# A macaron transformer layer on one core: probabilities turned by DMA, the work listed by slots, rotation on VectorE, halves of the weighted values summed by TensorE

## The chip, the core and the metric

The kernel runs on one core of a Trainium2 chip. The metric is the device time of one execution in microseconds. The kernel before takes 887.43 us as the median of three runs (884.81 to 891.82).

## What is computed

Sixteen sequences (batches) of 256 rows and 256 features go through half a feed-forward step, an attention step and half a feed-forward step. Every step normalises its input first and adds its result to the rows.

```python
def _layernorm(x, axis=-1, eps=1e-05):
    m = jnp.mean(x, axis=axis, keepdims=True)
    v = jnp.var(x, axis=axis, keepdims=True)
    return (x - m) / jnp.sqrt(v + eps)

def _L0_attn_ref(x, wq, wk, wv, wo):
    B, S, E = x.shape                       # 16, 256, 256
    H, D = (NUM_HEADS, HEAD_DIM)            # 16, 16
    q = apply_rope((x @ wq).reshape(B, S, H, D))
    k = apply_rope((x @ wk).reshape(B, S, H, D))
    v = (x @ wv).reshape(B, S, H, D)
    scores = jnp.einsum('bqhd,bkhd->bhqk', q, k) / math.sqrt(D)
    scores = scores + causal[None, None, :, :]
    attn = jax.nn.softmax(scores, axis=-1)
    return jnp.einsum('bhqk,bkhd->bqhd', attn, v).reshape(B, S, E) @ wo

def _L0_ffn_ref(x, W_up, W_gate, W_down):   # weights 1024 x 256, made ternary
    up = jnp.einsum('bsd,ed->bse', x, ternary_quant(W_up))
    gate = jnp.einsum('bsd,ed->bse', x, ternary_quant(W_gate))
    return jnp.einsum('bse,de->bsd', jax.nn.silu(up) * gate, ternary_quant(W_down))

x = x + 0.5 * _L0_ffn_ref(_layernorm(x), ...)
x = x + _L0_attn_ref(_layernorm(x), ...)
x = x + 0.5 * _L0_ffn_ref(_layernorm(x), ...)
```

Products run in float16. An operand that needs more bits is split into a high part (the value rounded to float16) and a low part (the rest), and both are multiplied.

## The kernel before

All 16 batches lie in SBUF. The unit of work is a **slot**. A full slot holds one **pair** of heads of one batch (128 pairs in all) and one **round** of a feed-forward step (two chunks of 128 hidden units; four rounds a step, 128 in all). Eight slots make a **step**, and in step t batch t is in its first feed-forward (slots 0 to 3), batch t-1 in its projections, batch t-2 in its pairs, and batch t-3 in its second feed-forward (slots 4 to 7). Each engine walks the steps with a list of its own (`PE_SLOT`, `ACT_SLOT`, `DVE_SLOT`, `POOL_SLOT` and the tables of exceptions `_OTHER` and `_EXTRA`), and engines wait for each other by counting semaphores. The order is thus written by hand.

What a **pair** does. TensorE writes the masked scores of both heads to PSUM: 256 columns for the upper half of the queries (rows 128 to 255) and 128 for the lower, since the mask is causal. VectorE takes the negated row maxima (`neg_max`, in SBUF) and multiplies them with the scale (`exp_bias`). ScalarE writes the exponentials (`prob`, float32, 384 columns a head). One slot later TensorE turns `prob` in three 128x128 transposes a head into `probt_ps` (one PSUM tile, so the heads go one after the other). ScalarE writes the high part `prob_h` and, for head 0, a float32 copy `prob_t`. The low part is made by GpSimd for head 0 (`prob_lo_0`, from the copy) and by VectorE for head 1 (`prob_lo_1`). Two slots after the scores TensorE multiplies with v: `v_row` holds per head 16 high columns, 16 low columns and a one, so 33 columns. VectorE inverts the sum (`pv_inverse`), adds the two halves of the weighted values (`pv_add`, into `pv_sum`) and multiplies (`pv_scale`, into `attn`).

What a **round** does. TensorE `up` (eight products of 256 columns) to ScalarE `tanh` to VectorE `silu`; TensorE `gate` (eight) and silu to VectorE `hidden`; ScalarE `hidden_hi` (`hid_h`) and GpSimd `hidden_lo` (`hid_l`); TensorE `down` (eight) in the next slot. `up_ps` and `gate_ps` are one tile each. `ffn_added` adds the sum of four rounds to the rows.

What a **batch** does beside that goes through one PSUM tile `misc_ps` in the order of the list `MISC`: the turning of the normalised rows for the three norms (norm1 and norm2 normalised by GpSimd in two operations, norm3 by VectorE), the projections of q and k (`qk0`, `qk1`: 12 products of 512 columns in all), of v, the turning of `attn` (`attn_t`) and `out_proj`. Of q and k ScalarE takes a copy (`qk_rows`), GpSimd multiplies it with cosine and sine (`rope_mul`, four operations of 512 columns a batch) and adds (`rope_add`); high and low parts go to `q_row` and `k_row`, and SP turns them by DMA (`turn_rows`) into `q_stk` and `k_pad`: 48 blocks of 128x128 a batch.

Within a slot `tanh` stands ahead of most exponentials on ScalarE, and the scores of the next pair wait until the exponentials of the last have read `score_ps`. This ring is scores, v's product, transposes, up, tanh, exponentials.

## Time and profile before

The profiled execution took 886.57 us, of which 884.8 us lie between its first and its last instruction (the span).

| | |
|---|---|
| median of the runs | 887.43 us |
| profiled execution | 886.57 us |
| its span | 884.8 us |
| TensorE busy | 708.4 us (80%), 6976 products |
| VectorE busy | 709.8 us (80%), 1591 instructions |
| ScalarE busy | 620.1 us (70%) |
| GpSimd busy | 557.4 us (63%) |
| DMA queue of SP | 109632 packets, 36.71 MB, 20.0% of 16 engines |
| mean granted TensorE clock | 0.951 |

A share of busy time says how close an engine is to being the limit, not that it is one: an engine that waits its turn in a ring shows as idle. Matmul durations overlap in TensorE's pipeline, so what a matmul costs is read from one start to the next.

### The profile page before, as it was taken

To read this page: it belongs to the slowest core of one execution; us is meant where nothing else is said; L and a number is where in the kernel's file an instruction comes from. 1 tells how busy PE (TensorE), PEld (TensorE's weight loads), DVE (VectorE), ACT (ScalarE), POOL (GpSimd) and SP (SyncE) were. 2 spreads that over 40 slices of the span, in tenths; PEclk is the share of its full clock that TensorE was granted. 3 is DMA by queue.
4 is the path that set the end of the run, shared out by engine and by line. 5 is a ranking of instruction groups with operands and counts; after the bars stand their busy time and mean duration, and the time that the engine had idled before them with its cause. 6 is when DMAs were issued, how large, how long until landed. Compare 5 with 4: busy or idle time off the path is not lost.

```text
span 884.8 us, 18797 instructions
## 1 busy us (share of the span) xinstructions
PE 708.4 (80%) x6976; PEld 584.6 (66%) x6976; DVE 709.8 (80%) x1591; ACT 620.1 (70%) x1365; POOL 557.4 (63%) x568
## 2 busy tenths in 40 slices
PE   0537578888888979898988888897979898767756
PEld 0325366777777868677777777786868777655544
DVE  2753486989998898988898999899898889777663
ACT  2104387878878788878887887878787788767642
POOL 2026685676768676767777676867676767744232
PEclk9968797999999999999999999999999999989798
DMA  8300312030303040302113030303040211213000
GB/s 317 119 1 1 72 29 45 13 66 9 73 13 73 14 72 13 72 14 48 39 21 65 1 73 14 72 14 73 14 72 14 55 31 31 55 29 57 1 13 13
DMA packets 110297, 40.20 MB, mean 45 GB/s; under 512 B 100992, under 2 KB 109440, under 8 KB 109696
## 3 DMA queue, kind: packets, MB, share of 16 engines
q1 hardware_dynamic: 109632, 36.71, 20.0%
q10 hardware_dynamic: 576, 2.29, 0.7%
q8 instruction: 57, 0.93, 0.4%
q14 instruction: 32, 0.26, 0.1%
HBM read 9.63 MB, written 4.19 MB: 16 GB/s over the span
## 4 chain that ended last, share of the span: by engine, by line
ACT 30%; PE 28%; DVE 19%; POOL 12%; issue 9%; DMA 1%; DVEq 0%; POOLq 0%; SPq 0%; ACTq 0%
PE misc_ps L386 7%; ACT prob L639 5%; ACT prob_h L630 5%; ACT tanh_b L648 5%; ACT prob L641 4%; PE pv_ps L435 4%; PE up_ps L386 3%; PE probt_ps L453 3%; POOL hid_l L1027 3%; DVE hid L934 3%; PE misc_ps L500 3%; ACT prob_t L634 3%; DVE silu_b L923 3%; PE score_ps L403 2%; POOL k_row L334 2%
## 5 line engine op out<-in xcount | busy, mean ns | idle before, releaser
L1027 POOL TENSOR_TENSOR hid_l<-hid,hid_h 128x512 f16<-128x512 f32 x128 | 148.5, 1161 | 225.9 <-ACT hid_h L654 210.9
L630 ACT ACTIVATE prob_h<-probt_ps 128x384 f16<-128x384 f32 x256 | 127.5, 498 | 76.5 <-PE probt_ps L453 76.2
L639 ACT ACTIVATE prob<-score_ps,exp_bias,exp_scale 128x256 f32<-128x256 f32 x256 | 147.2, 575 | 2.3 <-DVE exp_bias L874 1.2
L453 PE MATMUL probt_ps<-ident_f,prob 128*128 128x128 f32 x768 | 133.0, 283 | 13.8 <-ACT prob_t L634 13.8
L386 PE MATMUL up_ps<-xt_hi,tern_up 128*128 128x256 f16 x512 | 127.4, 286 | 20.2 <-DVE tern_up L708 13.1
L1020 POOL TENSOR_TENSOR prob_l<-prob_t,prob_h 128x384 f16<-128x384 f32 x128 | 118.1, 923 | 37.0 <-ACT prob_t L634 36.8
L386 PE MATMUL down_ps<-tern_down,hid_h 128*128 128x256 f16 x512 | 121.0, 276 | 19.3 <-POOL hid_l L1027 19.2
L386 PE MATMUL up_ps<-xt_lo,tern_up 128*128 128x256 f16 x512 | 127.4, 286 | 0.0
L386 PE MATMUL gate_ps<-xt_hi,tern_gate 128*128 128x256 f16 x512 | 123.9, 280 | 1.8 <-DVE tern_gate L708 1.8
L386 PE MATMUL gate_ps<-xt_lo,tern_gate 128*128 128x256 f16 x512 | 123.1, 279 | 0.0
L641 ACT ACTIVATE prob<-score_ps,exp_bias,exp_scale 128x128 f32<-128x128 f32 x256 | 121.2, 473 | 0.0
L386 PE MATMUL down_ps<-tern_down,hid_l 128*128 128x256 f16 x512 | 121.0, 276 | 0.0
L923 DVE SCALAR_TENSOR_TENSOR silu_b<-tanh_b,up_ps 128x512 f32<-128x512 f32 x128 | 87.0, 679 | 40.7 <-ACT tanh_b L648 40.2
L654 ACT ACTIVATE hid_h<-hid 128x512 f16<-128x512 f32 x128 | 82.8, 647 | 45.5 <-DVE hid L934 45.5
L648 ACT ACTIVATE tanh_b<-up_ps,tanh_scale 128x512 f32<-128x512 f32 x128 | 88.4, 690 | 33.0 <-PE up_ps L386 32.9
L868 DVE TENSOR_REDUCE neg_max<-score_ps 128x2 f32<-128x512 f32 x128 | 87.4, 683 | 22.5 <-PE score_ps L409 22.4
L453 PEld LDWEIGHTS probt_ps<-ident_f,prob 128*128 128x128 f32 x768 | 90.0, 144 | 21.4 <-issue 17.1
L934 DVE SCALAR_TENSOR_TENSOR hid<-silu_b,gate_ps 128x512 f32<-128x512 f32 x128 | 88.0, 687 | 17.7 <-DVE silu_b L923 0.5
L403 PE MATMUL score_ps<-mask_b,ident_b 128*128 128x256 bf16 x256 | 72.3, 283 | 28.3 <-ACT prob L641 24.9
L435 PE MATMUL pv_ps<-v_row,prob_h 128*128 128x33 f16 x768 | 55.9, 179 | 41.1 <-issue 27.4
L435 PEld LDWEIGHTS pv_ps<-v_row,prob_h 128*128 128x128 f16 x768 | 47.9, 97 | 54.8 <-issue 36.7
L916 DVE TENSOR_TENSOR prob_l<-probt_ps,prob_h 128x384 f16<-128x384 f32 x128 | 70.5, 551 | 14.8 <-ACT prob_h L630 14.6
(101 smaller groups left out, 1868.4 us busy)
## 6 DMA issues: line engine op xcount, KB each, us to landing
xs<-x SPq DMA_DIRECT2D x16, 256.0 KB, 2.8
out<-xs SPq DMA_DIRECT2D x16, 256.0 KB, 2.1
raw_gate<-w_gate_t ACTq DMA_DIRECT2D x1, 1024.0 KB, 7.6
raw_up<-w_up_t SPq DMA_DIRECT2D x1, 1024.0 KB, 7.7
raw_down<-w_down_t SPq DMA_DIRECT2D x1, 1024.0 KB, 10.4
raw_w<-wqkvo ACTq DMA_DIRECT2D x1, 1024.0 KB, 12.5
cos<-rope_cos SPq DMA_DIRECT2D x1, 512.0 KB, 13.6
sin<-rope_sin SPq DMA_DIRECT2D x1, 512.0 KB, 14.4
```

Of the source, the lines that this page charges most:

```text
L386: mm = pe.matmul(dst, lhs, rhs, start=flags and n == 0, stop=n == len(pairs) - 1, skip_group_check=True)
L403: pe.matmul(score_ps[:, j, P:3 * P], ident_b[:, :], mask_b[:, :], start=True, stop=False, skip_group_check=True)
L435: mm = pe.matmul(dst, part[:, pair % 2, j, col * P:(col + 1) * P], v[:, keys, h, :], start=first, stop=True, skip_group_check=True)
L453: mm = pe.transpose(probt_ps[:, n * P:(n + 1) * P], prob[:, pair % 2, j, col * P:(col + 1) * P], ident_f[:, :])
L630: act.activation(prob_h[:, pair % 2, j, :], probt_ps[:, 0:384], ACT.Copy).then_inc(prob_h_done, 1)
L639: act.activation(prob[:, s % 2, j, 0:256], score_ps[:, j, 0:256], ACT.Exp, bias=exp_bias[:, j:j + 1], scale=exp_scale[:, :])
L641: act.activation(prob[:, s % 2, j, 256:384], score_ps[:, j, 256:384], ACT.Exp, bias=exp_bias[:, 2 + j:3 + j], scale=exp_scale[:, :]).then_ ...
L648: act.activation(tanh_b[:, :], up_ps[:, :], ACT.Tanh, scale=tanh_scale[:, :]).then_inc(tanh_done, 1)
L923: dve.scalar_tensor_tensor(out=silu_b[:, :], in0=tanh_b[:, :], scalar=1.0, in1=up_ps[:, :], op0=ALU.add, op1=ALU.mult).then_inc(silu_done, 1)
L934: dve.scalar_tensor_tensor(out=hid[:, s % 2, :], in0=silu_b[:, :], scalar=0.25 / X_SCALE ** 2, in1=gate_ps[:, :], op0=ALU.mult, op1=ALU.mu ...
L1020: pool.tensor_tensor(prob_l[:, pair % 2, 0, :], prob_t[:, pair % 2, :], prob_h[:, pair % 2, 0, :], ALU.subtract).then_inc(prob_l_done[0], 1)
L1027: pool.tensor_tensor(hid_l[:, s % 2, :, :].rearrange("p m n -> p (m n)"), hid[:, s % 2, :], hid_h[:, s % 2, :, :].rearrange("p m n -> p (m ...
```

## The change

The work is listed by a running slot number g instead of by steps, for all engines. Pair n has its scores in slot n. Its parts and its rounds stand as follows.

- The rounds of the first feed-forward of batches 0 to 5 (24 rounds) stand in slots -15 to 8, one after another (`AHEAD = 6`); of later batches b in slots 8(b-6)+17 to +20. The second feed-forward of batch b stands in slots 8b+13 to 8b+16. So slots 13 to 96 have a round each, slots 9 to 12 none, and from 97 on every second group of four has none.
- Probabilities are no longer turned by TensorE. In the next slot ScalarE makes the high part of all 768 columns of the pair in one operation, GpSimd the low part of all 768, and SP turns both (12 blocks) in one DMA into `prob_t`. v's product comes three slots after the scores (`PV_LAG = 3`) instead of two.
- v's product is done in two: 17 columns (high part and the one) and 16 columns (low part), both summed into the same 17 columns of PSUM. There are 24 small products a pair instead of 12, and `pv_add` is gone; `pv_scale` reads PSUM.
- The scores of a half of the queries are one product for both heads (512 and 256 columns, with one product for the mask each). `neg_max` lies in a free corner of the scores' PSUM tile.
- VectorE multiplies q and k with cosine and sine straight from PSUM; the copy by ScalarE is gone.
- `up_ps` and `tanh_b` have two buffers, as the turned rows of norm1 have.
- The order within a slot is one list per engine without exceptions.

```diff
+PE_SLOT = ["scores", "product_v", "misc_a", "up", "gate", "misc_b", "down"]
+ACT_SLOT = ["prob_hi", "misc_a", "tanh", "exps_0", "exps_1", "rope_hi", "misc_b", "hidden_hi"]
+DVE_SLOT = ["row_max", "exp_bias", "pv_inverse", "ffn_added", "pv_scale", "misc_a", "norm_stats", "silu",
+            "norm_mean", "hidden", "norm_var", "norm_apply", "misc_b"]
+POOL_SLOT = ["norm_power", "rope_add", "prob_lo", "row_lo", "norm_apply", "hidden_lo"]
...
+            def turn_probs(n):
+                sp.wait_ge(prob_l_done, n + 1)
+                if n >= 2:
+                    sp.wait_ge(pv_done, n - 1)
+                sp.dma_start_transpose(prob_t[:, n % 2, :, :, :].rearrange("p a c q -> p (a c) q"),
+                                       prob_hl[:, n % 2, :, :].rearrange("p a k -> p (a k)")
+                                       ).then_inc(prob_turned[n % 2], 16)
...
-                            for part in (prob_h, prob_l):
-                                mm = pe.matmul(dst, part[:, pair % 2, j, col * P:(col + 1) * P], v[:, keys, h, :],
-                                               start=first, stop=True, skip_group_check=True)
+                            for part in range(2):
+                                p, head = prob_t[:, n % 2, part, block, :], v[:, keys, 2 * s + j, :]
+                                pe.matmul(dst, p, head[:, 0:HD + 1], start=first, stop=True, skip_group_check=True)
+                                mm = pe.matmul(dst[:, 0:HD], p, head[:, HD + 1:VW], start=False, stop=True,
+                                               skip_group_check=True)
...
+            def exps(n, tile):
+                act.wait_ge(bias_done, n + 1)
+                if tile and n >= 2:
+                    act.wait_ge(prob_l_done, n - 1)
...
+            def prob_hi(n):
+                act.wait_ge(exp_done[0], n + 1)
+                act.wait_ge(exp_done[1], n + 1)
+                if n >= 2:
+                    act.wait_ge(prob_turned[n % 2], 16 * (n // 2))
+                act.activation(prob_hl[:, n % 2, 0, :], prob[:, n % 2, :], ACT.Copy).then_inc(prob_h_done, 1)
...
+                    dve.tensor_tensor(rope_c[:, tile, :], misc_ps[:, :], cos[:, tile, :], ALU.mult)
+                    dve.tensor_tensor(rope_s[:, tile, :], misc_ps[:, :], sin[:, tile, :], ALU.mult
+                                      ).then_inc(misc_taken, 1)
...
-                dve.tensor_tensor(prob_l[:, pair % 2, 1, :], probt_ps[:, 0:384], prob_h[:, pair % 2, 1, :],
-                                  ALU.subtract).then_inc(prob_l_done[1], 1)
...
+            def norm_power(k, b):
+                pool.wait_ge(var_done[k], b + 1)
+                pool.tensor_tensor(rstd[k][:, :], var_s[k][:, :], minus_half[:, :], ALU.pow).then_inc(rstd_done[k], 1)
...
+            def prob_lo(n):
+                pool.wait_ge(prob_h_done, n + 1)
+                pool.tensor_tensor(prob_hl[:, n % 2, 1, :], prob[:, n % 2, :], prob_hl[:, n % 2, 0, :], ALU.subtract
+                                   ).then_inc(prob_l_done, 1)
```

How the rows move on GpSimd, around norm1 and norm2 of a steady batch (slots 5, 6 and 7 of a step). Before, `rstd` of the one norm stands behind a low part and its two applying operations follow in the next slot, and so for the other norm:

```order
L1020 TENSOR_TENSOR prob_l<-prob_t,prob_h 128x384
L977 TENSOR_TENSOR rstd<-var_s,minus_half 128x2
L1027 TENSOR_TENSOR hid_l<-hid,hid_h 128x512
L984 TENSOR_TENSOR centred<-xs,mv 128x512
L988 TENSOR_TENSOR xhat<-centred,rstd 128x512
L1020 TENSOR_TENSOR prob_l<-prob_t,prob_h 128x384
L977 TENSOR_TENSOR rstd<-var_s,minus_half 128x2
L1027 TENSOR_TENSOR hid_l<-hid,hid_h 128x512
L984 TENSOR_TENSOR centred<-xs,mv 128x512
L988 TENSOR_TENSOR xhat<-centred,rstd 128x512
L1020 TENSOR_TENSOR prob_l<-prob_t,prob_h 128x384
L1027 TENSOR_TENSOR hid_l<-hid,hid_h 128x512
```

After, in the places 5 to 7 of a batch, both `rstd` stand at the head of slot 6, ahead of the low part of pair 5 (`prob_hl` is now high and low part in one tensor), and the four applying operations of both norms stand together in slot 7:

```order
L912 TENSOR_TENSOR hid_l<-hid,hid_h 128x512
L871 TENSOR_TENSOR rstd<-var_s,minus_half 128x2 x2
L907 TENSOR_TENSOR prob_hl<-prob,prob_hl 128x768
L912 TENSOR_TENSOR hid_l<-hid,hid_h 128x512
L907 TENSOR_TENSOR prob_hl<-prob,prob_hl 128x768
L876 TENSOR_TENSOR centred<-xs,mv 128x512
L880 TENSOR_TENSOR xhat<-centred,rstd 128x512
L876 TENSOR_TENSOR centred<-xs,mv 128x512
L880 TENSOR_TENSOR xhat<-centred,rstd 128x512
L912 TENSOR_TENSOR hid_l<-hid,hid_h 128x512
L907 TENSOR_TENSOR prob_hl<-prob,prob_hl 128x768
L912 TENSOR_TENSOR hid_l<-hid,hid_h 128x512
```

The low part of the pair has moved behind `rstd`, which waits for VectorE's `var_s` of the same slot.

How they move on VectorE around norm3. Before, from the last row of slot 2 to `silu` and `hidden` of slot 3:

```order
L857 SCALAR_TENSOR_TENSOR v_row<-misc_ps,v_row 128x32x16
L868 TENSOR_REDUCE neg_max<-score_ps 128x2
L869 TENSOR_REDUCE neg_max<-score_ps 128x2
L807 BN_AGGR mv<-stats 128x2 x2
L886 RECIPROCAL inv_sum<-pv_ps 128x4
L813 TENSOR_SCALAR var_s<-mv 128x2
L874 TENSOR_SCALAR exp_bias<-neg_max,exp_scale 128x4
L893 TENSOR_REDUCE pv_sum<-pv_ps 128x64
L821 TENSOR_SCALAR xhat<-xs,mv,rstd 128x256 x2
L906 TENSOR_TENSOR attn<-pv_sum,inv_sum 128x2x32
L923 SCALAR_TENSOR_TENSOR silu_b<-tanh_b,up_ps 128x512
L934 SCALAR_TENSOR_TENSOR hid<-silu_b,gate_ps 128x512
```

After, from the `hidden` of place 3 to that of place 4 and what follows it:

```order
L832 SCALAR_TENSOR_TENSOR hid<-silu_b,gate_ps 128x512
L739 TENSOR_SCALAR var_s<-mv 128x2
L785 SCALAR_TENSOR_TENSOR v_row<-misc_ps,v_row 128x32x16
L796 TENSOR_REDUCE score_ps<-score_ps 128x2
L798 TENSOR_REDUCE score_ps<-score_ps 128x2
L803 TENSOR_SCALAR exp_bias<-score_ps,exp_scale 128x4
L809 RECIPROCAL inv_sum<-pv_ps 128x4
L817 TENSOR_TENSOR attn<-pv_ps,inv_sum 128x2x32
L823 SCALAR_TENSOR_TENSOR silu_b<-tanh_b,up_ps 128x512
L832 SCALAR_TENSOR_TENSOR hid<-silu_b,gate_ps 128x512
L745 TENSOR_SCALAR xhat<-xs,mv,rstd 128x256 x2
L762 TENSOR_TENSOR xt_lo<-misc_ps,xt_hi 128x512
```

The two `xhat` of norm3 have moved from ahead of silu and hidden to behind them, and `var_s` from ahead of exp_bias to the end of the slot before. On TensorE the transposes of norm3 stand in `misc_b`, now ahead of `down`; before, `down` stood ahead of them in that slot (`PE_OTHER[3]`).

How they move on SP, whose queue issues all turns. Before, a batch is one store and four turns:

```order
L374 DMA out<-xs 128x2x256 [waits ffn2_added]
L365 DMA_TRANSPOSE q_stk<-q_row 128x8x128 [waits scores_done,q_lo_done0]
L368 DMA_TRANSPOSE k_pad<-k_row 128x16x128 [waits k_lo_done0]
L365 DMA_TRANSPOSE q_stk<-q_row 128x8x128 [waits q_lo_done1]
L368 DMA_TRANSPOSE k_pad<-k_row 128x16x128 [waits k_lo_done1]
L374 DMA out<-xs 128x2x256 [waits ffn2_added]
```

After, the turns of eight pairs stand between them:

```order
L351 DMA out<-xs 128x2x256 [waits ffn_added_done]
L337 DMA_TRANSPOSE prob_t<-prob_hl 128x12x128 [waits pv_done,prob_l_done] x2
L325 DMA_TRANSPOSE q_stk<-q_row 128x8x128 [waits scores_done,q_lo_done0]
L328 DMA_TRANSPOSE k_pad<-k_row 128x16x128 [waits k_lo_done0]
L337 DMA_TRANSPOSE prob_t<-prob_hl 128x12x128 [waits pv_done,prob_l_done]
L325 DMA_TRANSPOSE q_stk<-q_row 128x8x128 [waits q_lo_done1]
L328 DMA_TRANSPOSE k_pad<-k_row 128x16x128 [waits k_lo_done1]
L337 DMA_TRANSPOSE prob_t<-prob_hl 128x12x128 [waits pv_done,prob_l_done] x5
```

Two of them stand around the turns of q and k, which wait for GpSimd's low parts in places 4 and 5.

## Rows read from the trace of the kernel before

**Rows 1.** Windows, steady stretch. Stretch, us, busy us (instructions) by engine, clock, DMA share, GB/s
```profile
380.00:700.00 320.00, 285.17 (x2918) 241.38 (x2917) 288.71 (x642) 255.58 (x569) 229.47 (x232) 0.98 0.19 37
```

**Rows 2.** Timeline, VectorE, L868. Start us, us, engine, line, operation, idle before
```profile
102.75 0.69 DVE L868 TENSOR_REDUCE neg_max<-score_ps 128x2 f32<-128x512 f32 x1 [2.52 <-PE score_ps L409]
...
192.15 0.69 DVE L868 TENSOR_REDUCE neg_max<-score_ps 128x2 f32<-128x512 f32 x1 [0.53 <-PE score_ps L409]
...
718.04 0.69 DVE L868 TENSOR_REDUCE neg_max<-score_ps 128x2 f32<-128x512 f32 x1 [0.53 <-PE score_ps L409]
...
841.29 0.69 DVE L868 TENSOR_REDUCE neg_max<-score_ps 128x2 f32<-128x512 f32 x1 [0.52 <-PE score_ps L409]
...
846.05 0.69 DVE L868 TENSOR_REDUCE neg_max<-score_ps 128x2 f32<-128x512 f32 x1 [0.52 <-PE score_ps L409]
```

**Rows 3.** Timeline, TensorE, a slot with one round and no projection
```profile
841.09 0.18 PE L435 MATMUL pv_ps<-v_row,prob_h 128*128 128x33 f16 x1
...
841.40 0.53 PE L453 MATMUL probt_ps<-ident_f,prob 128*128 128x128 f32 x3
841.76 0.27 PE L386 MATMUL up_ps<-xt_hi,tern_up 128*128 128x256 f16 x1
...
842.63 0.27 PE L386 MATMUL gate_ps<-xt_hi,tern_gate 128*128 128x256 f16 x1
```

**Rows 4.** Chain of waits, 437 to 442 us. Start us, us, what
```profile
439.10 0.38 ACT prob_h L630
...
439.86 0.57 ACT tanh_b L648
440.44 0.46 ACT prob L639
440.89 0.35 ACT prob L641
```

**Rows 5.** Groups by line and shape: xcount, busy us, mean ns, idle before and releaser
```profile
L1027 POOL TENSOR_TENSOR hid_l<-hid,hid_h 128x512 f16<-128x512 f32 x128 | 148.5, 1161 | 225.9 <-ACT hid_h L654 210.9 <-issue 14.6
...
L1020 POOL TENSOR_TENSOR prob_l<-prob_t,prob_h 128x384 f16<-128x384 f32 x128 | 118.1, 923 | 37.0 <-ACT prob_t L634 36.8
...
L923 DVE SCALAR_TENSOR_TENSOR silu_b<-tanh_b,up_ps 128x512 f32<-128x512 f32 x128 | 87.0, 679 | 40.7 <-ACT tanh_b L648 40.2
...
L916 DVE TENSOR_TENSOR prob_l<-probt_ps,prob_h 128x384 f16<-128x384 f32 x128 | 70.5, 551 | 14.8 <-ACT prob_h L630 14.6
...
L906 DVE TENSOR_TENSOR attn<-pv_sum,inv_sum 128x64 f32<-128x64 f32 x128 | 69.5, 543 | 6.9
...
L874 DVE TENSOR_SCALAR exp_bias<-neg_max,exp_scale 128x4 f32<-128x4 f32 x128 | 58.6, 458 | 0.8
...
L998 POOL TENSOR_TENSOR rope_c<-qk_rows,cos 128x512 f32<-128x512 f32 x32 | 40.7, 1270 | 1.8 <-ACT qk_rows L598 1.8
...
L984 POOL TENSOR_TENSOR centred<-xs,mv 128x512 f32<-128x512 f32 x32 | 33.3, 1041 | 0.0
```

**Rows 6.** Timeline, a steady batch, xhat of norm3 and its transposes
```profile
452.47 2.27 DVE L821 TENSOR_SCALAR xhat<-xs,mv,rstd 128x256 f32<-128x256 f32 x2 [0.49 <-POOL rstd L977]
...
454.88 0.63 PE L500 MATMUL misc_ps<-ident_f,xhat 128*128 128x128 f32 x4 [1.10 <-DVE xhat L821]
```

**Rows 7.** Timeline, the tail, the same two operations
```profile
861.74 0.73 DVE L821 TENSOR_SCALAR xhat<-xs,mv,rstd 128x256 f32<-128x256 f32 x2 [0.80 <-POOL rstd L977]
...
862.62 1.09 PE L500 MATMUL misc_ps<-ident_f,xhat 128*128 128x128 f32 x4 [3.75 <-DVE xhat L821]
```

**Rows 8.** Timeline, GpSimd, the head, after the maximum over the weights
```profile
51.12 2.26 POOL L1027 TENSOR_TENSOR hid_l<-hid,hid_h 128x512 f16<-128x512 f32 x2 [7.19 <-issue]
```

**Rows 9.** DMA: queue (packets, MB, share of 16 engines), then issues (us to landing)
```profile
q1 hardware_dynamic: 109632, 36.71, 20.0%
...
q_stk<-q_row SPq DMA_TRANSPOSE x32, 3.2
k_pad<-k_row SPq DMA_TRANSPOSE x32, 4.4
```

More of the change, by code:

```diff
@@ new lines @@
+PLAN = plan_rounds()
+ROUND_AT = {slot: (n, f, b, r) for n, (slot, f, b, r) in enumerate(PLAN)}
+FFN_ORDER = [(f, b) for _, f, b, r in PLAN if r == 0]
+FFN_START = {(f, b): slot for slot, f, b, r in PLAN if r == 0}
+FFN_ADD = {FFN_START[f, b] + ROUNDS + 1: (f, b) for f, b in FFN_ORDER}
+OF_BATCH = [("norm2", -8, "b"), ("qk0", -7, "b"), ("qk1", -6, "a"), ("v", -5, "b"), ("attn_t", 10, "b"),
+            ("out_proj", 11, "a"), ("norm3", 12, "b")]
+MISC = sorted([(SLOTS * b + at, place, what, b) for what, at, place in OF_BATCH for b in range(NBATCH)] +
+              [(FFN_START[1, b] - 1, "a", "norm1", b) for b in range(NBATCH)])
@@ L166, in macaron_kernel, with added, pair_at, batch_event @@
+def added(f, b):
+    return FFN_ORDER.index((f, b)) + 1
+def pair_at(slot):
+    return slot if 0 <= slot < PAIRS else None
+def batch_event(slot, table):
+    for at, value in table.items():
+        b, rest = divmod(slot - at, SLOTS)
+        if rest == 0 and 0 <= b < NBATCH:
+            return b, value
+    return None
+def run_slots(engine_slot, before={}):
+    for g in range(FIRST_SLOT, LAST_SLOT + 1):
+        if g in before:
+            before[g]()
+        engine_slot(g)
 def macaron_kernel(nc, x, wqkvo, w_up_t, w_gate_t, w_down_t, ident, mask, rope_cos, rope_sin, out):
@@ L413, in pair_of @@
[L413 to L427 removed]
+                        pe.wait_ge(stk_loaded[tile], 32 * (b + 1))
@@ L540, in misc @@
[L540 to L558 removed]
+                            xt_hi[2][:, 0, c, rows], xt_lo[2][:, 0, c, rows],
@@ new lines, in misc, with slot @@
+                mm.then_inc(misc_written, 1)
+            def slot(g):
+                for what in PE_SLOT:
+                    if what == "scores" and pair_at(g) is not None:
+                        scores(g)
+                    elif what == "product_v" and pair_at(g - PV_LAG) is not None:
+                        product_v(g - PV_LAG)
+                    elif what.startswith("misc"):
+                        for name, b in MISC_AT.get((g, what[-1]), []):
+                            misc(name, b)
+                    elif what == "up" and g in ROUND_AT:
+                        up(*ROUND_AT[g])
+                    elif what == "gate" and g in ROUND_AT:
+                        gate(*ROUND_AT[g])
+                    elif what == "down" and g - 1 in ROUND_AT:
+                        down(*ROUND_AT[g - 1])
```

825 lines of the change are left out of this document (329 added, 496 removed), and 6 rows, old and new, of the table ACT_OTHER.

## Prediction

> **What bounds the kernel now.** I read first the busy shares of a steady stretch: between 380 and 700 us TensorE is busy 285 of 320 us, VectorE 289, ScalarE 256, GpSimd 229 [rows 1]. No engine is full and two are near it, so the order of the waits decides, and the next thing to read is the time of a slot. The first row maximum of each pair's scores marks it [rows 2]: the first stands at 102.75 us, the last (pair 127) at 846.05, so 127 slots take 743.3 us. From 192.15 to 718.04 lie 88 slots, 11 batches of eight: 47.8 us a batch, 5.98 us a slot. Around this are a head of 102.75 and a tail of 884.8 - 846.05 = 38.75 us. A slot with one round and nothing else takes 846.05 - 841.29 = 4.76 us. What it is made of is read in TensorE's rows beside it [rows 3]: 12 products with v in 0.31 us, three transposes in 0.36, eight up products in 0.87 (0.109 each). The chain of waits gives ScalarE's steps from start to start [rows 4]: high part of 384 columns 0.38, tanh 0.57, exponentials 0.46 for 256 columns and 0.35 for 128.
>
> **The change, part by part.** I call a slot by its pair's place 0 to 7 in a batch.
> *TensorE* loses six transposes (0.72 us a slot) and gains 12 small products. Their price lies between nothing and the 0.026 us of the wider ones [rows 3]; I take 0.026, so 0.31. Saved: 0.4 us a slot.
> *ScalarE* loses three copies of 384 columns (1.14 us) and gains one of 768. Two of 384 make 0.76, one fixed cost less is below that; I take 0.8 since the source is wider than any row. The copy of q and k goes too.
> *VectorE* loses the low part (551 ns) and the sum of halves, and gains four rotation products of about 0.6 us a batch, a little under the 679 ns of silu, since one starts before the last ends [rows 5]. Its exp_bias (458 ns for four columns) and attn (543 ns for 64) are that long because they stand still while GpSimd runs [rows 5]: xhat takes 2.27 us for two in the steady part [rows 6] and 0.73 in the tail, where GpSimd is idle [rows 7]. Reading neg_max and the weighted values from PSUM may end this (0.25 us each) or not (as before); silu and hidden, with one operand in PSUM, show no such wait, so I take the first. Saved: about 1.1 us a slot.
> *GpSimd* gives up four rotation products (4 x 1.27 = 5.1 us a batch) and its low part grows from 384 to 768 columns. The rows at 384 (923 ns) and 512 (1161 ns) differ by 238 ns for 128 columns [rows 5], so 768 costs 1.64 us, 0.72 more a slot, 5.8 us a batch. It does not get lighter.
> *The turning by DMA*: 8 blocks land 3.2 us after issue, 16 in 4.4 [rows 9]; 12 give 3.8. From a pair's low part to its product with v lie about two slots less three microseconds, so it is covered in most places; where the low part is late, this comes on top. The queue was 20.0% busy for 768 blocks and the loads; 2304 blocks make about 50%, enough room.
>
> If only loads mattered, a bare slot would fall to 4.3 us: second scores 0.28, 24 products 0.6, up 0.87, 0.2 to its end, tanh 0.57, exponentials 1.6, 0.2 of hand-over. But two new orders stand in the batch, and I walked a steady batch operation by operation with the steps above.
>
> *Place 4 (norm3).* xhat now comes behind hidden on VectorE, and TensorE's transposes stand ahead of down and of the next scores. Gate ends 2.6 us into the slot; hidden ends 4.45 in; xhat then meets GpSimd's low part and q_row, as in [rows 6], and ends 7 in. TensorE idles 4.5 us; transposes 0.45, down 0.87 and first scores follow: 8.75 us.
> *Places 6, 7, 0.* GpSimd's two powers stand first in slot 6 but var comes at VectorE's end, 5.95 us in, behind ffn_added, four bn_stats, silu and hidden. From then GpSimd has no pause: powers 1.35, low part 1.62, hid_l 1.12, low part 1.62, two norm1/norm2 applications 4.25 (four of 1041 ns), hid_l 1.12: 17.05 us. Meanwhile exp waits for the low part two pairs back, down for hid_l (TensorE idles 3.1 us in slot 7), and v's product in slot 0 for a turn that lands at 12.8. Slot 1 begins at 18.35 us, where the bare three would take about 14.
> *Others*: 5.05 (place 1, q and k), 5.75 (2), 6.5 (3, TensorE full), 4.35 (5). Sum 8.75 + 18.35 + 5.05 + 5.75 + 6.5 + 4.35 = 48.75 us a batch.
>
> *The clock.* After 3.75 us of idleness in the tail four transposes take 1.09 us instead of 0.63 [rows 6, 7]: TensorE is granted its lower level, 1.2 instead of 2.4 GHz. Place 4 now leaves it idle for longer than that in each batch, and the work behind (about 2.5 us to the next tanh) would take up to 2 us more. Bounds 0 and 2; I take 1.25: 50 us a batch.
>
> *The sum.* Head: 15 rounds stand ahead of pair 0 instead of 8, in room where TensorE mostly waited; but the maximum over the weights stands behind two hid_l, and GpSimd's 7.19 us pause after it [rows 8] now delays the third down. I walk it to 108.5, bounds 102.75 and 115. Slots 0 to 8 (a round each, no attn_t) 48 us; 9 to 12 (no round, norm3 at 12) 20; 13 to 96 full: ten batches at 50 and four slots of 23 make 523; 97 to 127 (rounds in half the slots, no norm1; 40 us a batch by the same walk) 147; tail 38.75 + 2.5 for the turn in the last pair's path. Sum 108.5 + 48 + 20 + 523 + 147 + 41.3 = 887.8 us of span, against 884.8. The profiled execution took 886.57 us, 1.8 more than its span, and the median of the runs is 887.43. So 889.6, said as **890 us**: nothing that a measurement here (about 1%) can tell from no change.
>
> **Rivals.** *A, faster.* The loads decide. For it: three of four engines get lighter, and before, a bare slot waited for VectorE. If GpSimd does not hold xhat (0.73 instead of 2.5 us), the clock stays up and the chain 6-7-0 loses two of its four microseconds, a batch takes 48.75 - 1.75 - 2 = 45 us, the 84 slots 5 x 10.5 = 52 us less: 838 us. Against it: both orders are fixed in the lists.
> *B, slower, by the clock.* Both idle stretches of a batch are followed by the lower level through down, scores and v's products, at 2 us each, and once a batch in the slots from 97 on: 2.7 us more than forecast over 10.5 batches and 1.5 us in five others, 35 us: about 925 us. It passes the 1% bound from about 0.7 us a batch above my 50. For it: [rows 7]. Against: the stretch in slot 7 is 3.1 us, shorter than that row's.
> *C, the turn is late.* If landing takes 7 us rather than 3.8, slot 0's product waits 3.2 us longer, of which GpSimd's chain hides about half, and slot 3 and 4 go near their limit: about 2 us a batch, 910 us. For: k's and q's turns share SP's queue in places 4 and 5. Against: the shares above. The Trainium skill (VectorE: DVE Perf Modes, the three transpose paths) puts a 128x128 transpose at 1309 ns by DMA and 390 ns by TensorE; 12 in a row would make an estimated 15.7 us a pair and some 2010 us in all. The trace disagrees, with 16 blocks landed in 4.4 us [rows 9], so I give that form of C one chance in a hundred.
>
> **How the numbers follow.** Forecast (878 to 905 us) 0.42, A 0.33, B 0.20, C 0.05. Of the forecast 0.03 lies below 878.6 and 0.14 above 896.3: faster by over 1% 0.36, within 1% 0.25, slower 0.39. A's centre at 838 and B's with margin at 930 leave out about one in ten on each side.
>
> **What would show it.** Right: in the steady part GpSimd waits for var_s once a batch some 4 us; TensorE's transposes wait for VectorE's xhat for 3 to 5 us; slots near 5 us, with one over 8 and the three around norm1 over 17 together; the six-transpose group gone, exp_bias and attn near 250 ns, the 768-column low part 1.64 us. Wrong: no wait of TensorE above 2 us (then A), long waits for a DMA at v's product (C), a granted clock well under the present in the steady part (B). The forecast falls if a batch takes under 48 or over 52 us, or the first scores come before 100 us.

## The result: 2.65% slower, and the profile after

The changed kernel takes 911.53 us (median of four runs, 911.04 to 912.45); the kernel before took 887.93 us in the same comparison. The ratio is 1.0265, with a 95% interval of 1.0223 to 1.0307. It lies inside the stated range and 21.5 us above the forecast: my likeliest case (878 to 905 us) did not come, and the sign is that of rival B.

The profiled execution took 911.72 us, with a span of 909.9 us and a mean granted TensorE clock of 0.890 (before 0.951). TensorE is busy 699.4 us, VectorE 595.8, ScalarE 549.9, GpSimd 569.7: VectorE lost 114 us of work and ScalarE 70, and the kernel still got longer. The windows of the steady stretch, which answer to [rows 1] (us, then busy us and instructions of TensorE's products, its weight loads, VectorE, ScalarE and GpSimd, then clock, DMA share, GB/s):

```profile
380.00:700.00 320.00, 265.09 (x2885) 208.44 (x2884) 221.89 (x525) 209.68 (x419) 222.70 (x197) 0.88 0.56 101
```

Every engine is less busy than before and the clock fell from 0.98 to 0.88. The row maxima of pairs 0, 17, 89 and 127 (timeline, VectorE, L796), which answer to [rows 2]:

```profile
113.61 0.70 DVE L796 TENSOR_REDUCE score_ps<-score_ps 128x2 f32<-128x512 f32 x1 [1.54 <-PE score_ps L387]
...
206.35 0.70 DVE L796 TENSOR_REDUCE score_ps<-score_ps 128x2 f32<-128x512 f32 x1 [0.24 <-PE score_ps L387]
...
667.77 0.70 DVE L796 TENSOR_REDUCE score_ps<-score_ps 128x2 f32<-128x512 f32 x1
...
864.61 0.70 DVE L796 TENSOR_REDUCE score_ps<-score_ps 128x2 f32<-128x512 f32 x1 [0.55 <-PE score_ps L387]
```

The head grew from 102.75 to 113.61 us, the 127 slots from 743.3 to 751.0, the tail from 38.75 to 909.9 - 864.61 = 45.3: 10.9 + 7.7 + 6.5 = 25.1 us. A steady batch takes (667.77 - 206.35) / 9 = 51.27 us, 3.5 more than before; the slots from 97 on, half of which have no round, take 148.9 us instead of 170.7 and give most of it back.

The waits of the steady stretch (380 to 700 us; us in all, times, longest):

```profile
POOL rstd L871 <- DVE var_s L739: 45.2, 12, 3.8
...
PE misc_ps L455 <- DVE xhat L745: 29.3, 7, 4.2
...
PE down_ps L360 <- POOL hid_l L912: 15.6, 6, 2.6
...
PE pv_ps L408 <- DMA prob_t<-prob_hl: 3.6, 6, 0.8
```

The first three are the two new orders. The turn by DMA is the last and smallest of the four; ScalarE waits for it too, 8.9 us in six times, and e3 below tells what both waits are worth. GpSimd in places 6 and 7 of one batch (timeline):

```profile
393.05 1.15 POOL L912 TENSOR_TENSOR hid_l<-hid,hid_h 128x512 f16<-128x512 f32 x1 [1.14 <-ACT hid_h L595]
397.92 1.36 POOL L871 TENSOR_TENSOR rstd<-var_s,minus_half 128x2 f32<-128x2 f32 x2 [3.72 <-DVE var_s L739]
399.24 1.64 POOL L907 TENSOR_TENSOR prob_hl<-prob,prob_hl 128x768 f16<-128x768 f32 x1
400.84 1.15 POOL L912 TENSOR_TENSOR hid_l<-hid,hid_h 128x512 f16<-128x512 f32 x1
401.95 1.64 POOL L907 TENSOR_TENSOR prob_hl<-prob,prob_hl 128x768 f16<-128x768 f32 x1
403.55 1.04 POOL L876 TENSOR_TENSOR centred<-xs,mv 128x512 f32<-128x512 f32 x1
```

GpSimd stands 3.72 us for var_s while a low part (399.24) is queued behind the power, and then has no pause. TensorE, which waits for hid_l and xhat (timeline):

```profile
384.47 1.08 PE L455 MATMUL misc_ps<-ident_f,xhat 128*128 128x128 f32 x4 [4.19 <-DVE xhat L745]
385.35 0.42 PE L360 MATMUL down_ps<-tern_down,hid_h 128*128 128x256 f16 x1
385.56 0.42 PE L360 MATMUL down_ps<-tern_down,hid_l 128*128 128x256 f16 x1
...
390.75 0.27 PE L360 MATMUL down_ps<-tern_down,hid_h 128*128 128x256 f16 x1
390.86 0.27 PE L360 MATMUL down_ps<-tern_down,hid_l 128*128 128x256 f16 x1
...
402.04 0.28 PE L360 MATMUL down_ps<-tern_down,hid_h 128*128 128x256 f16 x1 [2.60 <-POOL hid_l L912]
...
402.71 0.27 PE L360 MATMUL down_ps<-tern_down,hid_h 128*128 128x256 f16 x1
402.82 0.35 PE L360 MATMUL down_ps<-tern_down,hid_l 128*128 128x256 f16 x1
402.96 0.42 PE L379 MATMUL score_ps<-mask_b,ident_b 128*128 128x256 bf16 x1
...
405.85 1.09 PE L455 MATMUL misc_ps<-ident_f,xhat 128*128 128x128 f32 x4 [0.42 <-POOL xhat L880]
...
409.28 0.42 PE L360 MATMUL gate_ps<-xt_hi,tern_gate 128*128 128x256 f16 x1
409.50 0.38 PE L360 MATMUL gate_ps<-xt_lo,tern_gate 128*128 128x256 f16 x1
409.71 0.28 PE L360 MATMUL gate_ps<-xt_hi,tern_gate 128*128 128x256 f16 x1
```

Products of 256 columns start 0.21 us apart behind the stretch of 4.19 us (the level of 1.2 GHz) and 0.11 apart at 390.75 (2.4 GHz). Behind the stretch of 2.60 us seven products of down still run at the upper level; then the lower one is granted, 0.8 us into the work, and the next four transposes take 1.09 us instead of the 0.63 of [rows 6]. It ends at about 409.7 us. In batches 3 to 10 each of the two stretches is followed by the lower level every time. (Below I count, place by place, the 16-bit products of 256 columns that last 0.42 us instead of 0.27: those ran at the lower level.)

The single prices, by group (xcount, busy us, mean ns, idle before and releaser), which answer to [rows 5], and the DMA's, which answer to [rows 9]:

```profile
L907 POOL TENSOR_TENSOR prob_hl<-prob,prob_hl 128x768 f16<-128x768 f32 x128 | 210.2, 1644 | 8.4 <-ACT prob_hl L586 8.4
L586 ACT ACTIVATE prob_hl<-prob 128x768 f16<-128x768 f32 x128 | 107.8, 842 | 24.2 <-DMA prob_t<-prob_hl 23.9
...
L817 DVE TENSOR_TENSOR attn<-pv_ps,inv_sum 128x64 f32<-128x64 f32 x128 | 28.5, 223 | 4.6
L803 DVE TENSOR_SCALAR exp_bias<-score_ps,exp_scale 128x4 f32<-128x4 f32 x128 | 28.4, 222 | 4.5
```

```profile
q1 hardware_dynamic: 310336, 87.06, 51.4%
...
prob_t<-prob_hl SPq DMA_TRANSPOSE x128, 3.8
```

### The profile page after: what moved, and what is told of

It reads as the page before. It is cut to its first block and busy times, and to the rows that moved or that the text cites. A ratio compares the mean times of both kernels' runs of the same rounds, so it can differ in the third digit from the quotient of the medians.

```text
span 909.9 us, 19277 instructions
## 1 busy us (share of the span) xinstructions
PE 699.4 (77%) x7488; PEld 537.7 (59%) x7488; DVE 595.8 (65%) x1399; ACT 549.9 (60%) x1077; POOL 569.7 (63%) x504
## 3 DMA queue, kind: packets, MB, share of 16 engines
q1 hardware_dynamic: 310336, 87.06, 51.4%
HBM read 9.63 MB, written 4.19 MB: 15 GB/s over the span
## 5 line engine op out<-in xcount | busy, mean ns | idle before, releaser
L575 ACT ACTIVATE prob<-score_ps,exp_bias,exp_scale 128x256 f32<-128x256 f32 (+1 forms) x512 | 219.2, 513 | 41.2 <-POOL prob_hl L907 27.5
L907 POOL TENSOR_TENSOR prob_hl<-prob,prob_hl 128x768 f16<-128x768 f32 x128 | 210.2, 1644 | 8.4 <-ACT prob_hl L586 8.4
L796 DVE TENSOR_REDUCE score_ps<-score_ps 128x2 f32<-128x512 f32 x128 | 89.1, 696 | 62.8 <-PE score_ps L387 62.3
L871 POOL TENSOR_TENSOR rstd<-var_s,minus_half 128x2 f32<-128x2 f32 x48 | 33.1, 699 | 148.9 <-DVE var_s L739 148.9
L586 ACT ACTIVATE prob_hl<-prob 128x768 f16<-128x768 f32 x128 | 107.8, 842 | 24.2 <-DMA prob_t<-prob_hl 23.9
L455 PE MATMUL misc_ps<-ident_f,xhat 128*128 128x128 f32 x192 | 41.4, 356 | 98.9 <-DVE xhat L745 66.9
L408 PE MATMUL pv_ps<-v_row,prob_t 128*128 128x17 f16 x1536 | 95.3, 172 | 12.7 <-DMA prob_t<-prob_hl 12.5
L408 PEld LDWEIGHTS pv_ps<-v_row,prob_t 128*128 128x128 f16 x1536 | 89.8, 98 | 24.0 <-DMA prob_t<-prob_hl 22.3
L409 PE MATMUL pv_ps<-v_row,prob_t 128*128 128x16 f16 x1536 | 94.0, 171 | 0.0
L360 PEld LDWEIGHTS down_ps<-tern_down,hid_h 128*128 128x128 f16 x512 | 52.2, 102 | 61.7 <-POOL hid_l L912 50.4
## 6 DMA issues: line engine op xcount, KB each, us to landing
raw_down<-w_down_t SPq DMA_DIRECT2D x1, 1024.0 KB, 10.9
```

Source lines behind the costliest of these rows:

```text
L360: mm = pe.matmul(dst, lhs, rhs, start=flags and n == 0, stop=n == len(pairs) - 1, skip_group_check=True)
L408: pe.matmul(dst, p, head[:, 0:HD + 1], start=first, stop=True, skip_group_check=True)
L409: mm = pe.matmul(dst[:, 0:HD], p, head[:, HD + 1:VW], start=False, stop=True, skip_group_check=True)
L575: e = act.activation(prob[:, n % 2, at + j * width:at + (j + 1) * width], score_ps[:, 1 - tile, j * width:(j + 1) * width], ACT.Exp, bias= ...
L586: act.activation(prob_hl[:, n % 2, 0, :], prob[:, n % 2, :], ACT.Copy).then_inc(prob_h_done, 1)
L796: dve.tensor_reduce(neg_max[:, 0:2], score_ps[:, 0, :].rearrange("p (j n) -> p j n", j=2), AX.X, ALU.max, negate=True)
```

## The experiments

Theory 1: the power at the head of GpSimd's list costs the time. Theory 2: the turn by DMA does. Theory 3: norm3's order does (its transposes ahead of down), by TensorE's wait for xhat and the lower clock behind it. The theory of the clock goes across 1 and 3: what the orders cost is largely the lower clock behind the stretches they leave. The first four and e9 are the changed kernel with one edit; ratios are to the kernel before on the same chip.

### e1_power: the power behind the low part

```diff
-POOL_SLOT = ["norm_power", "rope_add", "prob_lo", "row_lo", "norm_apply", "hidden_lo"]
+POOL_SLOT = ["rope_add", "prob_lo", "row_lo", "norm_power", "norm_apply", "hidden_lo"]
```

> The changed kernel, with GpSimd's power behind the low parts of its slot instead of at its head. GpSimd stood still there 45.2 us in 12 waits in 320 us, 7.5 us a batch of 51.3, and the low part of the probabilities queued behind it. Theory 1 (the order of the power costs): one low part of 1.64 us leaves the chain of places 6, 7 and 0, and the low part in place 3 comes earlier, so 2 to 3.5 us a batch, times some 14 batches 28 to 49 us less: 865 to 885 us, and the wait of TensorE for hid_l in place 7 (2.6 us) goes. Theory 2 (the turn by DMA costs) and theory 3 (the wait for xhat and the clock behind it cost): under 0.7 us a batch, 902 to 911 us.

Measured: 857.22 us, ratio 0.9634 (0.9609 to 0.9660): 54 us less than the changed kernel, and faster than the kernel before. The batch falls to 47.59 us. Theory 1 holds, with more than it asked for. The windows of its steady stretch and two of its waits:

```profile
380.00:700.00 320.00, 271.63 (x3127) 216.89 (x3125) 233.22 (x568) 227.79 (x455) 238.62 (x209) 0.94 0.59 107
```

```profile
POOL rstd L871 <- DVE var_s L739: 19.0, 13, 2.1
...
PE down_ps L360 <- POOL hid_l L912: 6.6, 8, 1.0
```

TensorE's wait for hid_l, 2.6 us long at most, is now 1.0 at most, and the clock rose from 0.88 to 0.94, which my expectation had left out: the second idle stretch is gone, and with it the 7 us at the lower level behind it. The gain in clock is not whole. TensorE now waits 1.6 us in place 0 for GpSimd's xhat, and in 4 of 8 batches about 3 us at the lower level follow (46 of 216 products in place 0, where the changed kernel has 112).

### e2_down: down ahead of norm3's transposes

```diff
                 for what in PE_SLOT:
+                order = PE_SLOT
+                if any(name == "norm3" for name, _ in MISC_AT.get((g, "b"), [])):
+                    order = PE_SLOT[:-2] + ["down", "misc_b"]
+                for what in order:
```

> The changed kernel, with TensorE's down ahead of norm3's transposes in the slots that have them, as the kernel before had it. TensorE stood still there 4.2 us a batch. If this order costs (theory 3), the 0.87 us of down (1.2 at the lower clock) move into the idle stretch, the rest of it is 3.1 us, and the work behind it at the lower clock is shorter: 1 to 2 us a batch, 15 to 30 us less: 882 to 897 us. If the place of down is free because the chain xhat, transposes, xt_hi sets the next round's up either way, 0 to 0.4 us a batch: 905 to 912 us.

Measured: 891.66 us, ratio 1.0024 (1.0009 to 1.0040): 20 us less, as theory 3 expected. The steady wait for xhat went from 29.3 us (longest 4.2) to 11.7 (longest 2.0), and place 4 from 8.88 to 7.58 us. Place 0, which the edit does not touch, falls from 8.07 to 7.20: TensorE still waits 2.60 us in place 7 of every batch, but the lower level follows in only 3 of 8. With this order alone put back, the change would have been worth nothing either way.

### e3_noturn: the turn left out

```diff
-                pe.wait_ge(prob_turned[n % 2], 16 * (n // 2 + 1))
+                pe.wait_ge(prob_l_done, n + 1)
...
-                                p, head = prob_t[:, n % 2, part, block, :], v[:, keys, 2 * s + j, :]
+                                p, head = prob_hl[:, n % 2, part, block * P:(block + 1) * P], v[:, keys, 2 * s + j, :]
...
-                if n is not None:
-                    turn_probs(n)
...
-                    act.wait_ge(prob_turned[n % 2], 16 * (n // 2))
+                    act.wait_ge(pv_done, n - 1)
```

> The changed kernel without the turning of the probabilities: v's product reads the unturned high and low parts as soon as they are made, so the attention is not computed; the number and the shape of the products stay, and SP issues 128 transposes of 12 blocks less. This is the whole price of the turn. If the turn costs (theory 2), 2 us or more a batch and its part in the tail, 30 us less or more: 881 us or under. If it is hidden (theories 1 and 3), only the last pair's landing and what v's product waited for it (3.6 us in 320) go: 4 us at the end and 0.6 a batch, 899 to 908 us.

Measured: 906.83 us, ratio 1.0179 (1.0139 to 1.0219). All 128 turns cost 4.7 us by the medians and 7.6 by the two ratios; a steady batch takes 51.27 us with them and without them. In the two profiled executions slots 97 to 127 take 144.5 us instead of 148.9 and the tail 1.0 us less, so what the turn costs lies where the slots are short. Theory 2 falls.

### e4_warm: the idle stretches filled

```diff
+            def fill(count):
+                for _ in range(count):
+                    pe.matmul(misc_ps[:, 0:256], ident_b[:, :], mask_b[:, 0:256], start=True, stop=True,
+                              skip_group_check=True)
...
+                    if k == 3:
+                        fill(34)
                     pe.wait_ge(xhat_done[k], b + 1)
...
                     elif what == "down" and g - 1 in ROUND_AT:
+                        if g >= 15 and g % SLOTS == 7 and g in ROUND_AT:
+                            pe.wait_ge(misc_taken, sum(at <= g for at, _, _, _ in MISC))
+                            fill(20)
```

> The changed kernel with idle products of 256 columns added on TensorE, into misc_ps while it is free: 34 (3.7 us) once a batch ahead of the wait for norm3's xhat, and 20 (2.2 us) ahead of down in place 7 of the slots with a round. They fill the two idle stretches of 4.2 and 2.6 us. If the lower granted clock behind each stretch is on the path (theory of the clock), it stays at its upper level, the steady part rises from 0.88 to 0.94 or more, and a batch loses 1.2 to 3 us: 20 to 40 us less, 870 to 892 us. If the stretches cost and the clock behind them doesn't, the time stays within 4 us of the changed kernel's or grows by up to 10 us through products that run over.

Measured: 882.56 us, ratio 0.9922 (0.9894 to 0.9950): 29 us less with 864 products more. The windows and a wait of its steady stretch:

```profile
380.00:700.00 320.00, 296.66 (x3455) 241.37 (x3453) 236.28 (x565) 224.92 (x447) 232.33 (x203) 0.99 0.60 107
```

```profile
POOL rstd L881 <- DVE var_s L749: 45.2, 13, 3.8
```

GpSimd still waits as long for var_s, and both orders are as they were; the clock is at 0.99 and a batch takes 48.31 us. So 2.96 us a batch of the changed kernel is the lower clock itself: 1.8 of it in places 4 and 5, behind the first stretch, and 1.1 in places 7 and 0, behind the second.

### e5_before_power: the order of the power in the kernel before

```diff
-    (6, "silu"): ["var_2"],
+    (6, "prob_lo_1"): ["var_2"],
...
-    ["apply_1", "prob_lo", "pow_2", "hidden_lo"],
+    ["pow_2", "apply_1", "prob_lo", "hidden_lo"],
```

> The kernel before, given one of the two new orders alone: in slot 6 of a step GpSimd's power for norm2 stands at the head of its list, ahead of norm1's application and of the low part of the probabilities, and the variance that it waits for is made behind hidden on VectorE. Leaving this order out of the changed kernel made it 54 us faster. If the order itself costs that (whatever else the kernel does), the kernel before gets slower by 2 to 4 us in each of about 16 steps: 915 to 950 us. If it is only dear together with the low part of 768 columns and the turn by DMA, 888 to 900 us, since here GpSimd's low part has only 384 columns and stands for one head.

Measured: 933.93 us, ratio 1.0545 (1.0525 to 1.0565). One moved word for GpSimd and one for VectorE cost the kernel before 48 us; a batch takes 51.26 us, and the slot that holds the wait 9.84 instead of 5.63. Its waits:

```profile
PE pv_ps L435 <- POOL prob_l L1020: 24.8, 13, 2.9
...
POOL rstd L977 <- DVE var_s L813: 19.9, 12, 2.8
```

The order costs by itself, without the turn and with low parts of 384 columns.

### e6_power_down: both orders put back

The edits of e1 and e2 together.

> The changed kernel with both orders put back: GpSimd's power behind the low parts (54 us alone) and TensorE's down ahead of norm3's transposes (20 us alone). They act in other places of a batch (7 and 0, and 4), so if each cost is its own, they add up but for the share of the clock: 835 to 845 us, and a batch of 45 to 46.5 us. If both were paid through the same thing (the lower granted clock behind a stretch of idleness, 29 us in all by the filled stretches), the sum saturates: 850 to 857 us.

Measured: 846.43 us, ratio 0.9551 (0.9527 to 0.9575). Alone they gave 54 and 20 us, together 65: mostly each its own, with 9 us shared, between the two expectations. Most of what is shared lies in place 0: e1 saves 0.44 us there and e2 0.87, both together only 0.22, and 81 of 216 products run at the lower level (e1 46, e2 29). Of the 4.55 us a batch that the two orders cost (51.27 to 46.72) at least 1.6 are not the clock, since a batch of e4, with the clock up and both orders in, takes 48.31. "Largely the clock" holds for e2's part more than for e1's: in place 7 the filling saves 0.4 us and e1 2.0.

### e7_head: the maxima over the weights earlier

```diff
+                weight_maxima()
                 dve.wait_ge(abs_all, 2)
                 scales(slice(2, 3))
...
-            run_slots(slot, before={FIRST_FFN: sum_all, FIRST_FFN + 2: max_all})
+            run_slots(slot, before={FIRST_FFN: sum_and_max_all})
```

Base: e6. `sum_and_max_all` calls the two reductions one after the other.

> The kernel of both orders put back, with the weights' maxima made ahead of the last ternary matrix on VectorE, and GpSimd's reduction over the partitions of them directly behind that of the sums. In the head of the changed kernel VectorE waits 8 us ahead of the third silu for that reduction, and GpSimd then 7.2 us ahead of norm1 of batch 1, and between the second and the fourth silu lie 22.6 us. If these two pauses set the head (which came 5 us above the forecast), the first scores' maximum comes 8 to 12 us earlier than at 113 and the whole time falls by as much. If the head is set by the 15 rounds on the engines, it falls by 3 us at most.

Measured: 836.97 us, ratio 0.9441 (0.9405 to 0.9476), 9.5 us less. The heads of GpSimd and VectorE in the changed kernel, then of GpSimd in e7 (timelines):

```profile
39.47 1.15 POOL L912 TENSOR_TENSOR hid_l<-hid,hid_h 128x512 f16<-128x512 f32 x1
46.51 0.39 POOL L943 PARTITION_ALL_REDUCE w_max_all<-w_max  x1 [5.88 <-issue]
53.89 1.03 POOL L876 TENSOR_TENSOR centred<-xs,mv 128x512 f32<-128x512 f32 x1 [7.00 <-issue]
```

```profile
46.93 0.17 DVE L690 TENSOR_SCALAR w_max<-w_max_all 128x4 f32<-128x4 f32 x1 [8.25 <-POOL w_max_all L943]
48.04 0.69 DVE L823 SCALAR_TENSOR_TENSOR silu_b<-tanh_b,up_ps 128x512 f32<-128x512 f32 x1
```

```profile
30.87 0.39 POOL L951 PARTITION_ALL_REDUCE w_max_all<-w_max  x1 [1.99 <-DVE w_max L689]
39.16 1.14 POOL L916 TENSOR_TENSOR hid_l<-hid,hid_h 128x512 f16<-128x512 f32 x1 [7.90 <-issue]
...
42.10 1.03 POOL L880 TENSOR_TENSOR centred<-xs,mv 128x512 f32<-128x512 f32 x1
```

Between a reduction over the partitions and an ordinary operation GpSimd pauses both ways: 5.88 us ahead of it and 7.00 behind. Side by side the two reductions share one such pair. The first row maximum comes at 98.3 us instead of 110.15. (The profiled execution of e7 took 831.8 us, 5 less than its median.)

### e8_head_apply: xhat of norm3 ahead of silu

```diff
-DVE_SLOT = [..., "pv_scale", "misc_a", "norm_stats", "silu", "norm_mean", "hidden", "norm_var", "norm_apply", "misc_b"]
+DVE_SLOT = [..., "pv_scale", "misc_a", "norm_apply", "norm_stats", "silu", "norm_mean", "hidden", "norm_var", "misc_b"]
```

Base: e7.

> The kernel of the run before in this call, with norm3's xhat made ahead of norm_stats and silu on VectorE instead of behind hidden. This is the other half of the new order of norm3. If TensorE's wait for it (24 us in 320 with the power put back) is on the path, 1.5 to 2.5 us a batch: 24 to 40 us less than that kernel. If silu and hidden behind it are then late by the same 2.3 us (two of xhat held by GpSimd's operations), nothing or a loss of up to 10 us.

Measured: 822.97 us, ratio 0.9294 (0.9264 to 0.9323): 14 us less, between the two expectations. Place 4 falls from 6.68 to 6.05 us, which is what the wait for xhat loses: in each of batches 3 to 10 it is 1.95 us instead of 2.57 (the longest of the stretch, 3.5, stands in no steady batch). Against e7 place 0 is 0.34 us shorter too, and place 5 0.46; fewer of their products run at the lower level (28 and 29 of 216, e7 57 and 75).

### e9_power12: only the powers of norm1 and norm2 behind

```diff
-POOL_SLOT = ["norm_power", "rope_add", "prob_lo", "row_lo", "norm_apply", "hidden_lo"]
+POOL_SLOT = ["norm_power_3", "rope_add", "prob_lo", "row_lo", "norm_power_12", "norm_apply", "hidden_lo"]
```

> The changed kernel with GpSimd's powers of norm1 and norm2 (slot at place 6) behind the low part, and that of norm3 (place 3) left at the head of its slot. It splits the 54 us of the first run. If the chain of places 6, 7 and 0 carries the cost, as the prediction walked it, 40 to 54 us of it are won here: 857 to 871 us. If the power at the head in place 3, which the prediction did not price, has half of it, 880 to 890 us. Place 7 should fall from 6.25 to 4.25 us in either case; place 4 stays at 8.9 if its delay is that of norm3's power and falls to 7.9 if it comes from elsewhere.

Measured: 870.29 us, ratio 0.9813 (0.9768 to 0.9857): 41 of the 54 us come from places 6 and 7. Place 4 stays at 8.88 us, where e1 has 7.89: the other 13 us are norm3's power at the head in place 3, which delays xhat (TensorE's longest wait for it is 4.2 us here and 3.5 in e1). A steady batch accounts for half of them (48.24 us for 47.59); slots 97 to 127 take 148.0 us and in e1 139.7.

### e10 to e12: the fastest kernel without the turn, with norm1 spread, with the wait filled

e10 is the edit of e3 on e8. e11 and e12, also on e8 (e12 fills the wait for norm3's xhat alone; of e4's second edit only the wait for `misc_taken` is in it, with no products):

```diff
-              [(FFN_START[1, b] - 1, "a", "norm1", b) for b in range(NBATCH)])
+              [(FFN_START[1, b] - (1 if b < AHEAD else 2), "a", "norm1", b) for b in range(NBATCH)])
...
+                    if k == 3:
+                        fill(20)
                     pe.wait_ge(xhat_done[k], b + 1)
```

> The fastest kernel so far (823 us: both orders put back, xhat of norm3 early, maxima early) without the turning of the probabilities by DMA: v's product reads the unturned parts, so the attention is not computed. Whether the turn was hidden only by the two idle stretches. If it was, the slots that are short now (4.25 us) wait for it, and without it the time falls by 15 us or more: 808 or under. If it is hidden by itself (3.8 us of landing against two slots of 4.25 less the parts' 2.5), 2 to 8 us: 815 to 821.

Measured: 821.73 us, ratio 0.9275 (0.9229 to 0.9320), 1.2 us under e8, which is not clear of noise, and less than either expectation: the turn is hidden in the short slots of a steady batch too.

> The fastest kernel so far with norm1 of the batches from 6 on one slot earlier, so that its statistics, power, application and transposes no longer share their slots with norm2's. If two applications in one slot on GpSimd (4.2 us beside a low part of 1.64) still hold places 7 and 0, place 0 falls from 7.3 us to about 6 and place 7 grows by less: 1 us a batch, 10 us less, 813 us. If all three engines are near their loads there, the same work lies in other slots for the same time: within 4 us of 823.

Measured: 829.17 us, ratio 0.9350 (0.9316 to 0.9383): neither expectation, 6 us slower. Place 0 falls to 4.90 us, but place 7 grows from 4.30 to 8.72: TensorE now waits there for GpSimd's xhat, 12.1 us in five times (2.4 a batch; in e8 it was 1.6, in place 0), and the lower level follows it: 108 of 216 products of place 7. How the 6 us split between the longer wait and the clock was not separated.

> The fastest kernel so far with 20 idle products of 256 columns (2.2 us) on TensorE ahead of the wait for norm3's xhat, which is 2.3 to 3.5 us long there. In the changed kernel filling both stretches gave 29 us. If the lower clock follows such a wait here too (steady part granted 0.97), it rises to 0.99 and 0.3 to 0.6 us a batch are won: 814 to 819 us. If the clock doesn't fall behind stretches of this length, the time is the same or up to 4 us longer.

Measured: 816.17 us, ratio 0.9210 (0.9172 to 0.9249): the fastest, 7.9% under the kernel before. The clock of its steady stretch is 0.99 (e8: 0.97), a batch 44.83 us (45.15).

## Why the prediction was off, step by step

Spacing of the row maxima by place, in us, mean over eight batches (pairs 24 to 88); "walk" is the prediction's, without its clock term, which gave 18.35 for places 6, 7 and 0 together.

| place | walk | after | e4 (filled) | e1 (power) | e2 (down) | e6 (both) | e8 |
|---|---|---|---|---|---|---|---|
| 1 | 5.05 | 5.03 | 4.95 | 4.99 | 4.94 | 5.04 | 4.95 |
| 2 | 5.75 | 6.18 | 6.27 | 6.18 | 6.31 | 6.18 | 6.21 |
| 3 | 6.5 | 7.11 | 7.12 | 7.12 | 7.11 | 7.11 | 7.12 |
| 4 | 8.75 | 8.88 | 7.55 | 7.89 | 7.58 | 6.68 | 6.05 |
| 5 | 4.35 | 4.69 | 4.26 | 4.53 | 4.83 | 4.66 | 4.30 |
| 6 | | 4.96 | 4.96 | 4.96 | 4.97 | 4.96 | 4.96 |
| 7 | | 6.25 | 5.86 | 4.24 | 6.12 | 4.27 | 4.30 |
| 0 | | 8.07 | 7.39 | 7.63 | 7.20 | 7.85 | 7.29 |
| 6+7+0 | 18.35 | 19.28 | 18.21 | 16.83 | 18.29 | 17.08 | 16.55 |
| 17 to 89, a batch | 48.75 | 51.27 | 48.31 | 47.59 | 48.99 | 46.72 | 45.15 |

Of span the forecast was 887.8 and 909.9 came. The 22.1 us are: head +5.1 (113.6 for 108.5), slots 0 to 8 +1.4, slots 9 to 12 +0.4, slots 13 to 96 +9.3 (532.3 for 523), slots 97 to 127 +1.9, tail +4.0 (45.3 for 41.3).

- **The walk of a batch came out right as a sum.** The two waits are where it put them (3.8 us of GpSimd for var_s, 4.2 of TensorE for xhat), and with the clock held up by e4 a batch takes 48.31 us against 48.75 walked. Its parts err both ways. Place 4 was walked at 8.75 us with the upper level, and with the clock held up it is 7.55; place 2 is 6.2 for 5.75 and place 3 7.11 for 6.5. In one place 3 TensorE is busy 6.97 of 7.11 us, and nothing done to the other engines moved it in any run, so there TensorE is the bound.
- **The clock was the mis-sized term of the steady part.** I took 1.25 us a batch, with bounds of 0 and 2, all of it behind the stretch in place 4; e4 measured 2.96, of which 1.8 stand there, inside the bounds, and 1.1 behind the stretch in place 7, which I had put at nothing. The failed step is the sentence that argued against B, that the stretch in slot 7 is shorter than that of [rows 7]. It was (2.60 us), and the lower level followed it all the same. B's mechanism is what happened, at 1.5 us a stretch on average rather than 2, and from there its 925 us against 911.5. I had also charged the lower level only to the work directly behind the wait; the rows show it from 402.8 to about 409.7 us, through the scores and transposes of place 0.
- **The turn costs little.** It lands in 3.8 us at 51.4% of the queue, as forecast, and all of it is worth 5 to 8 us (e3), or nothing clear of noise (e10). The Trainium skill (VectorE: DVE Perf Modes, the three transpose paths) gives 1309 ns for one block; twelve in a row would make an estimated 15.7 us, and the row disagrees. Rival C is refuted in both forms.
- **The prices of the parts held.** Low part 1.64 us as forecast, high part of 768 columns 0.84 for 0.8, exp_bias and attn 222 and 223 ns for 250. The reason given for the last two is in the traces: in the kernel before, the 23 of each that began while GpSimd had nothing in work took 225 and 216 ns, the 105 others 509 and 614; in the changed kernel both kinds take the same. A bare slot was put at 4.3 us; the last one of the changed kernel takes 4.27 (before 4.76). VectorE's and ScalarE's savings were real; they lie off the path as long as GpSimd's wait holds the chain.
- **The head was 5.1 us too short in my walk.** I charged the pause behind the reduction to the third down. What is late next is more: VectorE itself waits 8.25 us for that reduction ahead of its third silu, and then the application of norm1 of batch 1 waits through the 7.00 us pause, and TensorE's transposes behind it. e7 removed both and gained 11.9 us of head. But the head ends anywhere from 108.9 to 115.8 us in the six other kernels that keep this reduction in its place (e1 to e4, e6, e9), so how much of the 5.1 us is the walk's error stays open.
- **The tail was 4.0 us too short in my walk, and its one term too large.** It grew by 6.6 us, and I had put 2.5. The 2.5 us for the turn are 1.0 (tail 44.3 us without it in e3). But the last product with v stands three slots behind its scores and behind a down at the lower level: from the last row maximum to the first transpose of attn pass 12.9 us where 9.3 passed. Then the output projection runs at the lower level, as the chains of waits show (start us, us, what), first the changed kernel's and then that of the kernel before:

```profile
877.53 1.10 PE misc_ps L455 x4
...
880.04 2.75 PE misc_ps L360 x12
```

```profile
855.35 0.64 PE misc_ps L500 x4
...
857.39 1.50 PE misc_ps L386 x12
```

The two steps take 3.85 us instead of 2.14, 1.7 more. The remaining 1.2 stand at the end, most of them in the last down, 1.90 us instead of 1.06.

- **Not priced at all** was norm3's power at the head of place 3: 13 us of the 54 (e9 against e1).

- **Rival A's batch came once the orders were undone.** A had said 45 us a batch if the loads decide; e8 runs 45.15. That the two numbers agree is luck in part: A wanted xhat down to 0.73 us, and in e8 it still takes 2.2 (17.9 us for eight), with TensorE waiting for it in every batch.

What stays open: e1 saves 3.7 us a batch, 2.0 of them in place 7 and 1.0 in place 4. In place 7 the clock can have at most about the 0.4 us that the filling saves there; in place 4 the wait for xhat shrinks from 4.18 to 3.45 us, and how the rest splits was not separated. Nor does any run tell why the same stretch of 2.60 us is followed by the lower level in every batch of the changed kernel and in 3 of 8 in e2.
